# Rotary embedding of the second attention: the sine half moved from VectorE to ScalarE and GpSimd

## The reference, cut to what matters

```python
def apply_rope(x):                       # x: batch, head, position, 16 channels
    half = Dh // 2
    x1, x2 = x[..., :half], x[..., half:]
    return jnp.concatenate([x1 * cos - x2 * sin, x1 * sin + x2 * cos], axis=-1)

q = apply_rope(proj(query, Wq, bq))      # query: layernorm(x)
k = apply_rope(proj(key, Wk, bk))        # key, value: the context
v = proj(value, Wv, bv)
q = q * Dh ** (-0.5)
scores = where(mask, neg, einsum('bhqd,bhkd->bhqk', q, k))
out = einsum('bhqk,bhkd->bhqd', softmax(scores), v) @ Wo.T + bo
```

## Time and profile before

| | before |
|---|---|
| median of 3 runs | 1790.59 us (1787.74 to 1793.9) |
| the profiled execution, its own time | 1790.15 us |
| its span, first to last instruction | 1788.0 us |
| PE busy | 1587.2 us, 89% |
| DVE busy | 1237.1 us, 69% |
| ACT busy | 1002.6 us, 56% |
| GpSimd busy | 777.7 us, 43% |
| mean granted TensorE clock | 0.951 |

### The profile page before, as it was taken

One profiled execution on the slowest core, in us unless ns is written; L12 is line 12 of the kernel. 1 busy time (PEld: TensorE's weight loads), 2 busy tenths in 40 slices (PEclk: granted clock), 3 DMA queues, 4 the chain that ended last, 5 costly groups with the idle time before them and its releaser, 6 DMA issues. The chain is left out here.

```text
span 1788.0 us, 45017 instructions
## 1 busy us (share of the span) xinstructions
PE 1587.2 (89%) x16664; PEld 1228.1 (69%) x16664; DVE 1237.1 (69%) x3664; ACT 1002.6 (56%) x1742; POOL 777.7 (43%) x964
## 2 busy tenths in 40 slices
PE   4699999877899999999999578899887699999997
PEld 3355666546778888888888445666554388898874
DVE  4778888856446655555667478998988357757767
ACT  4377878664435444444533345676654358677752
POOL 4155657787320100010064443333465244677765
PEclk8799999999999999999999879999999799999999
DMA  5655646232164465355454243332333547799954
GB/s 161 142 119 119 137 111 139 55 109 83 50 205 152 145 200 188 117 185 195 128 157 133 65 101 81 73 70 57 67 79 88 204 141 238 234 299 289 314 176 141
DMA packets 297739, 257.03 MB, mean 144 GB/s; under 512 B 198079, under 2 KB 270187, under 8 KB 296248
## 3 DMA queue, kind: packets, MB, share of 16 engines
q1 hardware_dynamic: 271288, 168.84, 35.4%
q0 software_dynamic: 26240, 85.32, 14.6%
HBM read 102.98 MB, written 107.74 MB: 118 GB/s over the span
## 5 line engine op out<-in xcount | busy, mean ns | idle before, releaser
L1751 PE MATMUL ps<-m_xT,m_w_halves 128*128 128x256 f16 x3360 | 414.6, 273 | 0.0
L1751 PEld LDWEIGHTS ps<-m_xT,m_w_halves 128*128 128x128 f16 x3360 | 329.8, 98 | 39.5 <-ACT a_probs L1206 0.4
L1206 ACT ACTIVATE a_probs<-ps 128x1024 f32<-128x1024 f32 (+1 forms) x256 | 234.7, 917 | 164.8 <-PE ps L1033 161.5
L1782 PE MATMUL ps<-m_w_halves,m_hiddenT 128*128 128x256 f16 x1680 | 231.2, 274 | 14.8 <-DVE m_hiddenT L1911 12.1
L1836 ACT ACTIVATE m_hiddenT<-m_hidden 128x256 f16<-128x256 f32 x280 | 116.4, 416 | 210.8 <-DVE m_hidden L1906 209.2
L1330 POOL TENSOR_TENSOR a_probs<-a_probs,a_half_above 128x512 f32<-128x512 f32 x128 | 164.2, 1284 | 137.4 <-ACT a_probs L1206 136.8
L1033 PE MATMUL ps<-a_Q,a_K 32*128 32x256 f16 (+1 forms) x2048 | 147.0, 263 | 67.2 <-DVE a_neg_max L1424 30.2
L1911 DVE TENSOR_TENSOR m_hiddenT<-m_hidden,m_hiddenT 128x256 f16<-128x256 f32 x280 | 119.6, 427 | 124.8 <-ACT m_hiddenT L1836 124.6
L1702 POOL DMA_DIRECT2D expert_out<-m_y x40 | 29.1, 727 | 383.4 <-DVE m_y L1894 191.3
L1782 PEld LDWEIGHTS ps<-m_w_halves,m_hiddenT 128*128 128x128 f16 x1680 | 163.3, 98 | 40.0 <-DVE m_hiddenT L1911 17.5
L1427 DVE TENSOR_REDUCE a_qT<-ps 128x4 f16<-128x1024 f32 x128 | 156.7, 1224 | 48.1 <-PE ps L1044 47.1
(11 more groups left out here) (314 smaller groups left out, 3029.4 us busy)
## 6 DMA issues: line engine op xcount, KB each, us to landing
routed<-m_zeros POOLq DMA_DIRECT2D x32, 768.0 KB
r_space<-routed SPq DMA_DIRECT2D x48, 512.0 KB
routed_out<-m_y SPq DMA_DIRECT2D x48, 512.0 KB
r_w_load<-in_L_w SPq DMA_DIRECT2D x24, 896.0 KB, 7.2
dispatched<-r_x_halves SPq DMA_DIRECT2D x10, 1024.0 KB, 5.3
expert_out<-m_y POOLq DMA_DIRECT2D x40, 256.0 KB, 2.6
a_ctx_in<-in_ctx SPq DMA_DIRECT2D x32, 256.0 KB, 3.0
m_experts_load<-in_L_experts SPq DMA_DIRECT2D x18, 384.0 KB, 3.5
```

What stands on the lines that cost most here:

```text
L1206: A(pr[:, g % 2, 2 * jp:2 * jp + 2, :], SC[:, :, 0:SPAN], ACT.Exp, scale=1.0 / math.sqrt(DH)).then_inc(asem["ex"], 1)
L1751: last = mm(psum[:, v % HB, m * CH:(m + 1) * CH], wh[u][:, ws_, m, d_ * F0 + f_ * P:d_ * F0 + (f_ + 1) * P], xT[:, q % XB, xs_ * KT + d_, ...
L1782: last = mm(down_of(q, t), hT[:, hs_, f_, t * P:(t + 1) * P], wh[u][:, ws_, 2, f_ * D:(f_ + 1) * D], start=f_ == 0 and k == 0, stop=f_ == ...
```

## The change

`rotate` keeps the cosine product alone. A new ACT function `swapped` copies the same PSUM bank into the buffer `q_swapped` or `k_swapped` with the halves of each head exchanged, in two instructions, after the DVE's cosine product (semaphore `cosine`). GpSimd's `sums` first multiplies that buffer by the sine table in place, waits for its own product, and then adds. On ACT the copies stand in slot 5 (q) and at the end of slot 7 (k), and `upper_q` goes from slot 6 to slot 7. On GpSimd the sums of q go from slot 5 to slot 6, `lower_q` from 6 to 7, and the sums of k from slot 7 to slot 0 of the next iteration.

```diff
@@ scalar
+                def swapped(m, bank, r_, k, counter):
+                    need(act, "cosine", m, k)
+                    by_head = psum[:, bank, :].rearrange("p (t h d) -> p t h d", t=TT, d=DH)
+                    r4 = r_[:, :, :].rearrange("p t (h d) -> p t h d", d=DH)
+                    h8 = DH // 2
+                    A(r4[:, :, :, 0:h8], by_head[:, :, :, h8:DH], ACT.Copy)
+                    A(r4[:, :, :, h8:DH], by_head[:, :, :, 0:h8], ACT.Copy).then_inc(asem[counter], 1)
...
-                        if s == 6 and x3:
-                            if causal_band:
-                                upper_q(i + 3)
-                            else:
-                                upper_k(i + 3)
+                        if s == 5 and x3 and causal_band:
+                            swapped(i + 3, 4, qr, 0, "qrot")
+                        if s == 6 and x3 and not causal_band:
+                            upper_k(i + 3)
+                        if s == 7 and x3 and causal_band:
+                            upper_q(i + 3)
                         if s == 7 and o1:
                             need(act, "ont", i - 1)
                             need(act, "y", i - 2)
                             upper(oT[:, 0], 7, "oh")
+                        if s == 7 and x3 and causal_band:
+                            swapped(i + 3, 5, kr, 1, "krot")
@@ gpsimd
                 def sums(m, f_, r_, rot, ready):
                     need(pool, rot, m)
+                    r4 = r_[:, :, :].rearrange("p t (h d) -> p t h d", d=DH)
+                    pool.tensor_tensor(r4, r4, sin[:, :, :].unsqueeze(2).broadcast_to([P, TT, H, DH]), ALU.mult)\
+                        .then_inc(columns_set, 1)
+                    turns[0] += 1
+                    pool.wait_ge(columns_set, 2 + turns[0])
                     pool.tensor_tensor(f_[:, :, :], f_[:, :, :], r_[:, :, :], ALU.add).then_inc(asem[ready], 1)
...
                         if x3 and causal_band:
-                            if s == 5:
+                            if s == 6:
                                 sums(i + 3, qf, qr, "qrot", "qf")
-                            if s == 6:
+                            if s == 7:
                                 lower_q(i + 3)
-                            if s == 7:
-                                sums(i + 3, kf, kr, "krot", "kf")
+                        if s == 0 and x2 and causal_band:
+                            sums(i + 2, kf, kr, "krot", "kf")
@@ vector
-                    V.tensor_tensor(f4, by_head, table(cos, 0, DH), ALU.mult)
-                    V.tensor_tensor(r4[:, :, :, 0:h8], by_head[:, :, :, h8:DH], table(sin, 0, h8), ALU.mult)
-                    V.tensor_tensor(r4[:, :, :, h8:DH], by_head[:, :, :, 0:h8], table(sin, h8, DH), ALU.mult)\
-                     .then_inc(asem[counter], 1)
+                    V.tensor_tensor(f4, by_head, table(cos, 0, DH), ALU.mult).then_inc(asem["cosine"], 1)
```

## The result

The changed kernel took 1792.61 us (median of 12 runs, 1788.13 to 1800.37) beside 1787.12 us for the kernel before: ratio 1.0032 with the interval [1.0016, 1.0048], so slower by about 5.7 us. The profiled execution took 1793.95 us, with a span of 1792.1.

What follows compares the result with a forecast made beforehand. PE and DVE share the bound in the dense part, neither full alone. Losses 4.3 + 5.2 + 0.8 + 1.5 less 6.0 gain give 5.8 us, plus 1.5 clock: 1790.15 + 7.3 = 1797.5 us, range 1795.6 to 1802.

Steps and rivals of the forecast that it cites:

- Gathers: Last gather of each sequence leaves GpSimd ahead of `lower_q`, shortening DVE's waits for landings: 0.4 us each, 1.2 us gain.
- Relief of PE's waits for the maxima: Second attention: two fewer DVE instructions per rotation shorten PE's waits for DVE's maxima: 4.8 us gain, counted over six waits.
- GpSimd against DVE: Longer GpSimd work holds up DVE's routing pieces in iterations 8 and 12: 1.5 us loss, between 0 and 2 x 1.27.
- The second rival: The lock costs more, GpSimd's added work holding up DVE: 8.3 us on top, 1803 to 1810, say 1806; chance 0.13.
- ACT's order: `upper_q` ahead of oT delays k's copies and v projection: 5.2 us in iterations 5, 7, 9, 11; 0.8 in eight others.
- The filling: Iterations -3 to -1: k's copies stand behind `upper_q`, which waits for GpSimd, delaying the v projection: 4.3 us loss.
- My upper end, 6: Upper end for the loss in the filling: 6 us if its second step is paid again.
- The clock: More broken PE work in the filling and four pauses will not raise the granted clock: 1.5 us loss added.
- Durations: ACT's copies take 0.37 us, GpSimd's product 1.27; PE's 25.4 us of waits for the maxima fall to about 20.
- The rival that ended faster: DVE's relief pays where PE waits, if ACT ends k's copies before PE's slot 0 transposes are done: 1781.5 us; chance 0.10.

Runs made afterwards that it cites:

- experiment 9: The kernel before with one line moved, `lower_q` to slot 7 so that slot's gather is issued ahead of it, rotation unchanged: 1781.75 us, ratio 0.9971.
- q alone: The changed kernel with only q rotated in the new way, k keeping DVE's sine products and its old places: 1776.09 us, ratio 0.9939.
- experiment 2: The changed kernel with ACT's copies of k ahead of `upper_q` instead of behind it: 1793.22 us, ratio 1.0042.
- experiment 12: The changed kernel with q moved everywhere, k only in the sequences 9, 11, 13 and 15: 1782.42 us, ratio 0.9985.
- k alone: The changed kernel with only k rotated in the new way, q keeping the old rotation and its old places: 1782.83 us, ratio 0.999.
- experiment 1: The changed kernel with the first three sequences rotated and ordered as in the kernel before: 1790.71 us, ratio 1.0017.
- experiment 4: The changed kernel without GpSimd's product with the sine: 1777.78 us, ratio 0.9944.
- experiment 8: The kernel before without DVE's two sine products, GpSimd adding zeros instead: 1775.82 us, ratio 0.9929.

## Why the prediction came out near, and which of its steps were wrong

The forecast was a loss of 7.3 us on its own execution, measured were 5.7 on the medians and 3.8 on the profiled ones. That the sum held is luck in part: the gain from the gathers and the losses from GpSimd and from the filling were all put too small, with opposite signs. Term by term:

- **Gathers, 1.2 us of gain.** The step that failed worst. "0.4 us each is what I expect": the kernel before with only this edit (experiment 9) gained 9.1 us up to iteration 6 and 5.2 us (0.0029) in the median. I took 1.2 of the 4.9 us that DVE waits for landings. The trace had it: `lower_q` waits 1.26 or 1.27 us for ACT with a gather behind it, in each of the iterations -1 to 3, and 4.0 of the 4.9 us went out of PE's waits for the maxima.
- **Relief of PE's waits for the maxima, 4.8 us.** The line fell by 5.6 us, from 30.2 to 24.6, with the gathers' part and less what GpSimd holds up; 6.0 - 1.5 = 4.5 was the forecast for the three, so the net came out and its parts did not. Counting waits that follow a rotation was a poor measure of the relief: without the sine products and with nothing in their place the kernel gains 12.7 us, of which that line has 2.2 in the profile. In iterations 0 to 5 q's relief adds nothing measurable to the gather's: gains of 8.2 and 7.3 us.
- **GpSimd against DVE, 1.5 us of loss.** Mis-sized; the places were those I had named. The combine takes 949 ns instead of 613, and 18.2 us of DVE for its 20 instructions where q alone has 11.0. Iterations 0 to 5 gain 2.9 us where q alone gains 8.2: about 5 us, not "so little for the gathers". Without GpSimd's product the kernel is 15.7 us faster, which includes 3.9 of the filling. The second rival's mechanism was there, then, and its 8.3 us were nearer than my 1.5. The gathers, 5.2 us where I had 1.2, are a part of what kept the time from 1806; that they are all of it is not shown. The reads from PSUM were as free as I took them: L1464 takes 686 ns, L1450 took 685. The small operations even gained: the cast behind the maxima has a mean of 217 ns after and 304 before, L193 333 and 700 (1040 to 1345 us). That the moved sums no longer meet them is my reading, from the places of the instructions.
  The Trainium skill (SBUF — State Buffer, section "SBUF: two separate sides") speaks of an exclusive lock on a pair of ports that the two engines share. This trace agrees in both directions: two combines took 2.19 us for 0.88, and the four sums of k that ran beside a combine took 1.33 or 1.34 us where those of q take 1.26 to 1.28.
- **ACT's order, 5.2 + 0.8 us.** Right in place, name and size: four waits of 1.16 us and eight of 0.2 to 0.3 make 6.8. Against it stand 1.5 us of old waits for k at the same place. What I had not seen is that turning the order round doesn't help: then `upper_q` is late, and the kernel is no faster (experiment 2).
- **The filling, 4.3 us.** Right in mechanism, too small. The first v projection was 2.8 us late by my sum, waits 2.79 and starts 3.0 later, counted from the first `a_xn`; the first maxima come 3.4 us later (2.5 expected), the second v projection 6.4 (4.3), the first exponential's iteration 6.1 (4). My upper end, 6, "if the second step is paid again", is what happened: the row at 1031.00 waits 2.79 a second time. The clock adds to it: 12 matmuls in 2.08 us for 1.48. The old filling itself took 35.0 us in one execution and 32.6 in another.
- **The clock, 1.5 us of loss.** PE is busy for 307.5 us from iteration 0 to the last slot where it was busy for 304.1, with the same matmuls, 3.8 us more of it from iteration 13 on. But a fall of that kind comes and goes between executions of one code (experiment 12), so this term can be neither confirmed nor refuted.
- **Durations.** ACT's copies 378 to 386 ns (375 expected), GpSimd's product 1.27 us (1.27), PE's waits for the maxima less by 5.6 us (less by about 5).

The rival that ended faster had its point of decision in the wrong place: not whether ACT ends the copies of k before PE needs the bank, but whether k is moved on top of q at all. By the ratios, k costs 0.0039 early, 0.0044 late, and the first three sequences 0.0015: 0.9939 + 0.0098 = 1.0037, beside 1.0032 measured. Each of these prices is uncertain by about 0.003, so that the sum comes out this well is chance too.

## What to carry to other kernels

Before you price what an engine is relieved of, look at what each engine issues behind a wait: a DMA that stands behind an instruction that waits for another engine is late by that whole wait, and here one line that put the gather ahead gave about half of what moving q gave. Work moved to GpSimd was paid on DVE where DVE's additions, with their inputs in SBUF, ran beside it (949 ns for 613), and not where DVE read PSUM (686 for 685), so give it slots of the second kind, and ask for each moved piece alone whether it gains: here q alone gave 0.9939, k alone 0.999, both 1.0032. And a sum that comes out right proves none of its terms: the gathers' was off by 4 us, and GpSimd's product cost 15.7 us, 11.8 of them outside the filling, where 1.5 was put down. Compare the waits of two kernels between the same two instructions, not between the same two times.

## What the runs showed of the hardware that was not expected

- Two GpSimd instructions in a row can hold two of DVE's: beside a product and a sum, two combines of together 0.88 us took 2.19, and GpSimd's sum was stretched a little too (1.34 for 1.27).
- A wait of 2.79 us of PE in the filling was followed by matmuls at about 0.7 of their speed (12 in 2.08 us for 1.48), with a granted clock of 0.68 over the window; the same wait at 1031.00 was followed by 1.49. The mean clock of the whole execution is 0.951 in both kernels.
- The last iteration, with the same matmuls in every kernel, took 14.05 us at a granted clock of 1.00, 14.69 at 0.94 (the changed kernel) and 17.35 at 0.75. It had the long form in 4 of the 14 profiled executions (experiments 1, 4, 8 and 12).
- Executions of the same kernel differ by 15 us and more (1778.6 to 1793.74 for the kernel before on one chip), and most of it goes with the mean granted clock: 0.963 in the shortest of these 34 and 0.948 in the longest. In the three groups of 30 to 35 executions, 0.01 of clock goes with 7 to 8 us.
